# A decoder layer on one core: V as the stationary operand in 64-column tiles, probabilities normalised ahead of their transposes, long steps in parts, another step order

## The reference

```python
q = x_norm @ W_q;  k = ctx @ W_k;  v = ctx @ W_v          # 16 heads of 16
scores  = q @ k^T * 16 ** -0.5, masked keys at a very negative value
probs   = softmax(scores over the 77 keys)
x = x + concat_heads(probs @ v) @ W_proj + b_proj
```

## Time and profile before

| | value |
|---|---|
| median of three runs | 1521.48 us (1519.7 to 1524.4) |
| the profiled execution's own time | 1518.72 us |
| its span, first to last instruction | 1516.6 us |
| busy: PE / DVE / ACT / POOL | 96% / 80% / 63% / 55% |
| share of the chain that ended last | PE 91%, DVE 3% |
| granted TensorE clock, mean | 0.989 |

### The profile page before, as it was taken

One profiled execution on the slowest core, in us unless ns is written; L12 is line 12 of the kernel. 1 busy time (PEld: TensorE's weight loads), 2 busy tenths in 40 slices (PEclk: granted clock), 3 DMA queues, 4 the chain that ended last, 5 costly groups with the idle time before them and its releaser, 6 DMA issues.

```text
span 1516.6 us, 31405 instructions
## 1 busy us (share of the span) xinstructions
PE 1456.9 (96%) x10520; PEld 1291.4 (85%) x10520; DVE 1217.1 (80%) x3006; ACT 961.4 (63%) x2531; POOL 828.6 (55%) x937
## 2 busy tenths in 40 slices
...
GB/s 250 98 100 18 24 10 23 17 24 24 25 24 15 18 16 24 24 24 24 24 10 23 17 24 24 24 24 10 23 16 24 24 24 24 21 13 18 17 7 14
DMA packets 113102, 45.03 MB, mean 30 GB/s; under 512 B 86192, under 2 KB 109104, under 8 KB 112944
## 3 DMA queue, kind: packets, MB, share of 16 engines
...
## 4 chain that ended last, share of the span: by engine, by line
PE 91%; DVE 3%; issue 2%; POOL 1%; ACT 1%; DMA 1%; SPq 0%; POOLq 0%; DVEq 0%; ACTq 0%
PE bank L444 76%; PE bank L450 7%; PE bank L685 5%; PE bank L770 2%; PE bank L532 1%; DVE a_conv L887 1%; PE bank L738 0%; DVE a_rC L909 0%; ACT x_prob L1331 0%; SPq L433 0%; DMA x_prob<-in_ctxT 0%; DVE x_nmax L1013 0%; DMA x<-in_x 0%; PE bank L541 0%; DVE x L1035 0%
## 5 line engine op out<-in xcount | busy, mean ns | idle before, releaser
L1331 ACT ACTIVATE x_prob<-bank,x_nmax 128x77 f32<-128x77 f32 x1024 | 248.5, 329 | 51.2 <-DVE x_nmax L1013 50.2
L1013 DVE TENSOR_REDUCE x_nmax<-bank 128x4 f32<-128x308 f32 x256 | 120.1, 469 | 109.8 <-PE bank L444 106.0
L1344 ACT ACTIVATE x_probT<-bank 128x256 f32<-128x256 f32 (+1 forms) x256 | 112.2, 438 | 98.3 <-PE bank L685 98.1
L1497 POOL TENSOR_TENSOR a_orinv<-a_ove,mhalf 128x8 f32<-128x8 f32 x32 | 65.1, 2035 | 199.1 <-DVE a_ove L952 199.1
L444 PE MATMUL bank<-x_Vbd,x_probT 128*128 128x34 f32 (+1 forms) x1280 | 162.5, 267 | 0.7 <-DVE x_o L1027 0.7
L887 DVE SCALAR_TENSOR_TENSOR a_conv<-a_raw,cw,a_conv 128x256 f32<-128x256 f32 x384 | 155.0, 478 | 7.5 <-POOL a_conv L1459 7.5
L444 PEld LDWEIGHTS bank<-x_Vbd,x_probT 128*128 128x128 f32 x1280 | 158.0, 192 | 1.1 <-DVE x_o L1027 1.1
L685 PE MATMUL bank<-ident,x_prob 128*128 128x128 f32 x640 | 114.6, 277 | 0.4 <-ACT x_prob L1331 0.3
L909 DVE RECIPROCAL a_rC<-bank 128x512 f32<-128x512 f32 x32 | 107.1, 3348 | 0.6 <-PE bank L444 0.6
L912 DVE TENSOR_TENSOR a_AT<-bank,tri 128x512 f32<-128x512 f32 x128 | 87.7, 685 | 23.9 <-PE bank L444 23.9
L444 PE MATMUL bank<-x_K_bd,x_Q_stack 128*128 128x308 f32 x256 | 94.5, 369 | 8.6 <-ACT x_prob L1331 5.2
...
## 6 DMA issues: line engine op xcount, KB each, us to landing
...
x_Vbd<-v_tok SPq DMA_DIRECT2D x128, 9.6 KB
```

The costliest lines, as they stand in the source:

```text
L1013: dve.tensor_reduce(nmax[:, u % 2, :], X0[:, 0:UH * S2].rearrange("p (h s) -> p h s", h=UH), AX.X, ALU.min).then_inc(on.x_max, 1)
L1331: ins = act.activation(prob[:, col:col + S2], X0[:, i * S2:(i + 1) * S2], ACT.Exp, scale=-1.0, bias=nmax[:, u % 2, i:i + 1])
L1344: act.activation(probT[:, g[0]:g[-1] + 1, :].rearrange("p h t -> p (h t)"), X1[:, 0:len(g) * P], ACT.Copy).then_inc(on.x_pT, 1)
```

## The change

The product with V is turned round. `Vbd` now has no ones' columns and holds 64 columns (4 heads) for each of 6 slots and 2 head groups; it is the stationary operand, and `probT`, which now keeps all 256 tokens, streams with 256 columns. Heads of even quarters go to PSUM partitions 0 to 63, odd ones to 64 to 127: two 128 x 64 tiles of the array, addressed in turn. `x_av` has 2 steps of 6 matmuls for a row where it had 8 with 20 in all. The result is already features x tokens, so `x_ot` on TensorE and `x_o` on VectorE go. The sums are taken from the exponentials: per unit a VectorE sum (`x_sum`), a reciprocal (`x_rs`) and a GpSimd product (`x_nrm`) stand between `x_prob` and the transposes. The two loads of `vones` become two GpSimd memsets. `a_conv` is 6 steps of 2, `a_rc` 2 of 256 columns, `x_kbd` 6, `f_yy` 2. The order of the steps is new on every engine.

```diff
             def x_pt(r, u):
-                pe.wait_ge(on.x_prob, upto(r, NU, u + 1))
+                pe.wait_ge(on.x_nrm, upto(r, NU, u + 1))
                 if u > 0:
                     pe.wait_ge(on.x_pT, upto(r, NU, u))
-            def x_av(r, u):
-                c, q = divmod(u, QU)
...
-                for t in GROUPS[q]:
-                    h, w = first_head(t) * (HD + 1), tile_heads(t) * (HD + 1)
-                    ins = mm(X2[:, h:h + w], probT[:, t, :], Vbd[r % 2][:, t, 0:w], start=(t == 0),
-                             stop=(t == NT - 1))
+            def x_av(r, g):
...
+                pe.wait_ge(on.x_pT, upto(r, NU, QU + 2 * (g + 1)))
+                for j in range(VS // 2):
+                    for i in range(2):
+                        t = g * NT // 2 + 2 * i + j
+                        ins = mm(X2[i * VW:(i + 1) * VW, g * T:(g + 1) * T], Vbd[r % 2][:, g, i * VS // 2 + j, :],
+                                 probT[:, t, :], start=(j == 0), stop=(j == VS // 2 - 1))
                 ins.then_inc(on.x_av_ps, 1)
-            def x_ot(r):
-                pe.wait_ge(on.x_o, upto(r, TC))
-                turn(X1, xo).then_inc(on.x_oT_ps, 1)
...
-            def a_conv(r):
+            def a_conv(r, i, h):
                 dve.wait_ge(on.a_tap0, upto(r))
...
-            def a_rc(r):
+            def a_rc(r, c):
...
-                dve.reciprocal(flat(rC[r % 2]), E0[:, :]).then_inc(on.a_rC, 1)
+                dve.reciprocal(rC[r % 2][:, c, :], E0[:, c * D:(c + 1) * D]).then_inc(on.a_rC, 1)
...
+            def x_sum(r, u):
+                dve.wait_ge(on.x_prob, upto(r, NU, u + 1))
+                q = u % QU * UH * PITCH
+                dve.tensor_reduce(xsum[:, u % 2, :], prob[:, q:q + UH * PITCH].rearrange("p (h s) -> p h s", h=UH)[:, :, 0:S2],
+                                  AX.X, ALU.add).then_inc(on.x_sum, 1)
+
+            def x_rs(r, u):
+                dve.wait_ge(on.x_sum, upto(r, NU, u + 1))
...
+                dve.reciprocal(xrs[:, u % 2, :], xsum[:, u % 2, :]).then_inc(on.x_rs, 1)
...
+            def x_nrm(r, u):
+                pool.wait_ge(on.x_rs, upto(r, NU, u + 1))
+                q = u % QU * UH * PITCH
+                p = prob[:, q:q + UH * PITCH].rearrange("p (h s) -> p h s", h=UH)[:, :, 0:S2]
+                pool.tensor_tensor(p, p, spread(xrs[:, u % 2, :], S2), ALU.mult).then_inc(on.x_nrm, 1)
```

More of the change, by code:

```diff
@@ L62 @@
     "a_qnT a_P_ps a_P a_o_ps a_osq a_oss a_ove a_orinv a_o1 a_o2 a_oT_ps a_oT a_wo_ps a_x1 "
-    "g_ps g_hi g_lo g_v x_kbd x_q_ps x_q x_ql a_xnTl x_xnTl f_xnTl a_Ehi a_Elo a_oTl x_oTl f_sTl x_neg x_s_ps x_max x_prob x_pT_ps x_pT "
-    "x_av_ps x_rs x_o x_oT_ps x_oT x_x1b x_proj_ps x_x2 f_gate_ps f_lgT f_lg_ps f_logit f_top f_topi f_topf "
+    "g_ps g_hi g_lo g_v x_kbd x_q_ps x_q x_ql a_xnTl x_xnTl f_xnTl a_Ehi a_Elo a_oTl x_oTl f_sTl x_neg x_s_ps x_max x_prob x_sum x_rs x_nrm x_pT_ps x_pT "
+    "x_av_ps x_oT x_x1b x_proj_ps x_x2 f_gate_ps f_lgT f_lg_ps f_logit f_top f_topi f_topf "
     "f_gap f_egap f_gden f_gw1 f_gw2 f_wt12 f_wt f_u_ps f_v_ps f_th f_su f_s f_sw f_sT_ps "
@@ L181, in build @@
         KT_lo_bd = sb("x_KT_lo_bd", [P, KC, HB, S2], F32R)
[L182 to L183 removed]
+        Vbd = [sb(f"x_Vbd_{i}", [P, 2, VS, VW]) for i in range(2)]
         nmax = sb("x_nmax", [P, 2, UH])
         prob = sb("x_prob", [P, NH * PITCH])
[L186 to L188 removed]
+        probT = sb("x_probT", [P, NT, T])
+        xsum = sb("x_sum", [P, 2, UH])
+        xrs = sb("x_rs", [P, 2, UH])
         xoT = halves("x_oT", [P, KC, T])
```

192 lines of the change are left out of this document (82 added, 110 removed).

## The result

The changed kernel takes 1561.6 us (median of 4 runs, 1561.0 to 1566.6), the kernel before 1521.1 on the same chip: 1.027 times as long, 95% interval 1.0243 to 1.0297. The forecast was 1536, slower: the direction is right, the size isn't, 15 us forecast and 40 measured.

The account below looks back on a forecast made before the run. The prediction took TensorE, busy 96%, to bound the kernel before. Pieces of 2.0 + 3.2 + 7.75 + 3.3 + 27.9 = 44.15 us, 0.45 more a row, over 32 rows 14 us, gave 1533, median 1536 us; range 1486 to 1580.

Parts of the forecast that it names:

- The blocks: The new V products on TensorE, 24 passes a row: 2.9 us, 1.45 a block, assuming the two column tiles partly overlap.
- X1 stalls: TensorE waits for copies from the bank units 6 and 7 share: 0.65 us before unit 7, 0.35 before the second block.
- (e): Piece from `x_s` 2 to `a_ktok`: 27.9 us by VectorE's stream and GpSimd's operations behind it; TensorE's way 26.5 us.
- rival without overlap: The tiles' passes do not overlap: TensorE's way 28.8 to 29.6 us, pitch 45.05 to 45.85, 1565 to 1590 us; chance 0.15.
- (a): Piece from `a_ktok` to the next `a_A`: one transpose, 12 passes of `x_proj` and `a_vtok`, 2.0 us.
- (b): Piece from `a_A` to `x_q`: as before but without `a_turn`, which has moved, 3.2 us.
- (c): Piece from `x_q` to `x_s` 1: 7.75 us through ScalarE and VectorE, TensorE's own work 7.1, so it stalls 0.65.
- (d): Piece from `x_s` 1 to `x_s` 2: `x_s`, `a_v`, `f_u0` and a short wait for a copy, 3.3 us.
- the tail of (e): GpSimd's operations behind VectorE's stream, from `f_sw` to `a_kr`, before `a_ktok`: 6.8 us, with 0.2 for hand-overs.
- the 1.4 us of slack: Between `x_s` 2 and `a_ktok`, TensorE's way was put 1.4 us shorter than the way over VectorE and GpSimd.
- VectorE and GpSimd's tail as the new bound: The main forecast: VectorE's stream and GpSimd's operations behind it set the row, 1526 to 1550 us; chance 0.41.
- tiles overlap and TensorE stays the bound: Rival: VectorE's stream and GpSimd's operations behind it stay hidden, pitch 42.1 to 42.75, faster, 1470 to 1491 us; chance 0.27.

Follow-up runs that it names:

- tiles_serial: Changed kernel with the loops of a V block exchanged, the three products of one column tile before the three of the other: 1590.2 us.
- no_norm: Changed kernel without the normalisation's sums, reciprocals and products, the transposes waiting for the exponentials instead: 1559.5 us.
- x1_bank: Changed kernel with unit 7's transposes put into bank X0 in place of X1, no step moved: 1551.6 us.
- slot: Changed kernel with unit 7's transposes in bank X0, `a_rot` before the second `f_stl`, and `x_kbd` 0 before the second `f_sw`: 1534.5 us.

## Why the prediction was wrong in size

**TensorE's terms.** The blocks were costed 2.9 us a row and take 2.88; the overlap was assumed from no row, and the starts in pairs and tiles_serial show it. The X1 stalls were costed 0.65 and 0.35; by starts they are 0.79 and 0.31. TensorE's way through (e) was forecast at 26.5 us and is 28.0 up to one step behind the last `f_yy` (783.86 to 766.84 + 44.90 + 0.12). Of the 1.5 us missing, 0.37 is the wait for `f_sw` 0 and 0.47 are waits ahead of `x_s` 6 and 7, 0.23 and 0.24 by starts; the prediction has these only in its rival without overlap, as 0.8 us, and not in the 26.5 of the forecast. The rest is 0.1 at X1 and steps that cost more than the sum gave them. The prediction's own numbers disagreed here: by subtraction from the pitch it had 42.9 us for TensorE with the X1 stalls, by adding up the pieces 42.1.

**VectorE's load.** 40.2 forecast, 41.0 measured: an `x_rs` costs 0.09 and the sums 0.39 as summed; the excess is `a_silu_v`, 1.28 us in the mean (0.68 before), and the `conv`, 0.500 in place of 0.478.

**The walk.** (a) 2.0 forecast, 2.0 measured (767.31 to 769.31). (b) 3.2 and 3.37: `x_turn` waits for `x_xn`. (c) 7.75 and 7.76. (d) 3.3 and 3.42. (e) 27.9 and 28.35 (783.86 to 767.31 + 44.90). In (e) VectorE's stream was forecast 20.2 and took 20.3 (784.49 to 804.76, where the half `a_rC` behind it starts); the tail behind it was forecast 7.0 and took 7.4: `a_sin` waits for `a_rot`.

**The step that failed** is the tail of (e), and with it the 1.4 us of slack that the text gave TensorE's way there. It lists GpSimd's operations and leaves out what they wait for: `a_rot` stands on VectorE behind `f_stl`, which waits for ScalarE's copy of the second `f_st`, and that is what the X1 stalls make late. ScalarE, which the prediction costs at nothing because it is idle 14 us a row, stands in this chain and in the one ahead of the first `f_st`. So the way over TensorE and the way over VectorE's stream and GpSimd's tail meet in `a_sin`, and the one over TensorE, forecast 1.4 us shorter, is 0.31 us the longer. That the loop has no slack for TensorE is shown by tiles_serial (0.94 us more, 0.90 longer); that VectorE's added work isn't needed for the length by no_norm (2 us); that the X1 wait and the hand-overs behind it are, by x1_bank (10 us) and slot (27 us). Once the X1 stall is off, the next chain is 0.33 us shorter and holds the row; that one does run through VectorE's sums, `x_nrm` and GpSimd's tail. The forecast "VectorE and GpSimd's tail as the new bound" came within 0.45 us as a sum for (e) and was wrong as a cause; that its sum came so near is luck, since two ways of nearly the same length end there. The rival "tiles overlap and TensorE stays the bound" is wrong on the side of time.

**The sum.** 44.15 a row was forecast and 44.90 came. The pitch before was taken as 43.70; it alternates between 43.72 and 43.85, so 0.08 of the rise was none. 1.12 us over 31 rows are 35 us. The other 9 us the forecast didn't have at all: it multiplied the pitch by the rows and kept the ends. What makes the first three rows 15 us longer was not looked into and stays open.

**What would show it.** Pairs of V products that start together: they do. TensorE's idle time stands before unit 7's transposes and before `a_ktok`, released as named; before `x_s` 1 there is none in the rows of the matmuls, only 0.17 us in those of the weight loads, released by `x_prob`. The first `f_st` and `x_turn` have idle time that was not named.
